# Softmax of the final attention blocks: negated peak as bias of the exponential and per-head sums on ScalarE, with a new order table for those blocks

## The reference, cut to what matters

```
x = x + xattn(layernorm(x), ctx)           # 6 layers, 4 batches
x = x + attn(layernorm(x), ...)
x = x + ffn(layernorm(x), ...)

# attn, for each batch
scores  = einsum('bhse,bhte->bhst', q, k) / sqrt(8) + causal
weights = softmax(scores, axis=-1)
attn    = einsum('bhst,bhte->bshe', weights, v)

# ffn: c carries from batch to batch
ft = sigmoid(xt @ wf.T + c @ uf.T + bf);  it = sigmoid(...);  gt = tanh(...)
c  = ft * c + it * gt
```

## Time and profile before

| | |
|---|---|
| runs | 2611.82, 2612.84, 2605.08 us |
| profiled execution | 2607.36 us, span 2605.6 us |
| PE busy | 2482.2 us (95% of the span), 12652 matmuls |
| DVE busy | 2238.7 us (86%) |
| ACT busy | 2042.3 us (78%) |
| POOL busy | 604.8 us (23%) |
| granted TensorE clock | 0.976 of full over the span |

### The profile page before, as it was taken

One profiled execution on the slowest core, in us unless ns is written; L12 is line 12 of the kernel. 1 busy time (PEld: TensorE's weight loads), 2 busy tenths in 40 slices (PEclk: granted clock), 3 DMA queues, 4 the chain that ended last, 5 costly groups with the idle time before them and its releaser, 6 DMA issues.

```text
span 2605.6 us, 37962 instructions
## 1 busy us (share of the span) xinstructions
PE 2482.2 (95%) x12652; PEld 1522.6 (58%) x12652; DVE 2238.7 (86%) x4427; ACT 2042.3 (78%) x3861; POOL 604.8 (23%) x392
## 2 busy tenths in 40 slices
PE   4799999999999999999999999999999999999876
PEld 2456656656656656656666666566566566565554
DVE  6689898898898898898898898898988988988875
ACT  2588888888888888888888888888888888888531
POOL 3312312212213213213123123123122122131000
PEclk8799999999999999999999999999999999999986
DMA  3000010001001001001001001001001001000000
GB/s 129 25 9 17 25 36 17 25 9 38 25 7 46 17 9 47 9 17 52 9 17 46 9 17 52 9 17 46 9 17 52 9 17 46 9 1 26 1 1 5
DMA packets 16573, 63.56 MB, mean 24 GB/s; under 512 B 2241, under 2 KB 7410, under 8 KB 11642
## 3 DMA queue, kind: packets, MB, share of 16 engines
q1 hardware_dynamic: 16378, 61.13, 7.3%
HBM read 48.25 MB, written 0.29 MB: 19 GB/s over the span
## 4 chain that ended last, share of the span: by engine, by line
PE 58%; DVE 17%; ACT 13%; issue 8%; POOL 3%; DMA 0%; SPq 0%; ACTq 0%; DVEq 0%; POOLq 0%
PE psS L1052 16%; PE psO L1100 9%; PE psO L1101 9%; PE psO L1103 9%; ACT P L890 6%; ACT PH L887 5%; DVE PL L636 4%; PE psL L1146 3%; PE psL L1157 2%; PE psL L1052 2%; DVE back_x L709 1%; ACT qraw L909 1%; POOL back_rstd L422 1%; DVE V L686 1%; PE psA L1203 1%
## 5 line engine op out<-in xcount | busy, mean ns | idle before, releaser
L887 ACT ACTIVATE PH<-psS 128x512 fp32r<-128x512 f32 x1536 | 1009.4, 657 | 177.3 <-PE psS L1052 158.7
L636 DVE TENSOR_TENSOR PL<-P,PH 128x512 fp32r<-128x512 f32 x1536 | 1038.5, 711 | 94.5 <-ACT P L890 84.6
L890 ACT ACTIVATE P<-psS 128x512 f32<-128x512 f32 x1536 | 1009.3, 657 | 108.5 <-DVE PL L636 108.3
L1052 PE MATMUL psS<-QT,KT 128*128 128x512 f16 x3072 | 927.5, 384 | 0.5 <-ACT P L890 0.5
L1100 PE MATMUL psO<-PH,V 128*128 128x512 f32 x1536 | 876.4, 571 | 0.0
L1101 PE MATMUL psO<-PH,VL 128*64 128x512 f32 x1536 | 606.7, 395 | 0.0
L1103 PE MATMUL psO<-PL,V 128*128 128x512 f32 x1536 | 605.9, 394 | 0.1
L1052 PEld LDWEIGHTS psS<-QT,KT 128*128 128x128 f16 x3072 | 216.2, 100 | 368.4 <-issue 281.1
L1100 PEld LDWEIGHTS psO<-PH,V 128*128 128x128 f32 x1536 | 292.2, 190 | 178.0 <-ACT PH L887 9.8
L1103 PEld LDWEIGHTS psO<-PL,V 128*128 128x128 f32 x1536 | 288.1, 188 | 152.1 <-DVE PL L636 0.8
L422 POOL TENSOR_TENSOR rn<-ssc,neghalf 128x16 f32<-128x16 f32 (+2 forms) x73 | 240.7, 3298 | 347.6 <-DVE ssc L571 265.7
(11 more groups left out here) (365 smaller groups left out, 2835.0 us busy)
## 6 DMA issues: line engine op xcount, KB each, us to landing
ctx_sb<-ctxT SPq DMA_DIRECT2D x24, 1024.0 KB, 4.7
KT<-KT SPq DMA_DIRECT2D x48, 256.0 KB, 3.5
W<-wpack SPq DMA_DIRECT2D x6, 1280.0 KB, 5.3
W<-wpack SPq DMA_DIRECT2D x6, 1088.0 KB, 7.3
W<-wpack SPq DMA_DIRECT2D x6, 576.0 KB, 5.7
KT<-biasM SPq DMA_DIRECT2D x1, 1024.0 KB
W<-tail_w SPq DMA_DIRECT2D x1, 832.0 KB
P<-biasW SPq DMA_DIRECT2D x1, 512.0 KB
```

The lines of the kernel that those rows point to most:

```text
L636: nc_v.tensor_tensor(PL[:, here, :], P[:, t % PSLOTS, :], PH[:, here, :], ALU.subtract).then_inc(sem("p_lo"), 1)
L887: nc_a.activation(PH[:, t % HSLOTS, :], bank, ACT.Exp, scale=SIM_SCALE).then_inc(sem("p_hi"), 1)
L890: nc_a.activation(P[:, t % PSLOTS, :], bank, ACT.Exp, scale=SIM_SCALE).then_inc(sem("ca_exp"), 1)
L1052: ins = mm(bank, keys[part], q, start=(part == 0), stop=(part == 1))
```

## The change

The arithmetic stays the same. In the mask stage the subtraction over 128 x 512 goes, and a small instruction negates the four peaks (128 x 4) in its place. The exponential of a chunk, one instruction over 128 x 512 before, becomes four of 128 x 128, one a head; each takes its negated peak as bias and gives the row sum as accumulated output. The four sum stages are replaced by one, `sums`, which waits for the last exponential of the block and takes the reciprocal.

```diff
                         link(nc_v.tensor_reduce(t.peak[:, 4 * c:4 * c + 4], t.s[c], AX_X, ALU.max))
-                        nc_v.tensor_tensor(t.s[c], t.s[c], t.peak[:, 4 * c:4 * c + 4].unsqueeze(2).broadcast_to([128, 4, N]), ALU.subtract).then_inc(sem("t_sub"), 1)
+                        nc_v.tensor_scalar(t.peak[:, 4 * c:4 * c + 4], t.peak[:, 4 * c:4 * c + 4], -1.0, None, ALU.mult).then_inc(sem("t_peak"), 1)
...
-                def sums(c):
-                    def stage():
-                        dve.wait_ge(sem("t_exp"), t.b * 4 + c + 1)
-                        link(nc_v.tensor_reduce(t.sum[:, 4 * c:4 * c + 4], t.s[c], AX_X, ALU.add))
-                        if c == 3:
-                            link(nc_v.reciprocal(t.inv[:], t.sum[:]))
-                    return stage
+                def sums():
+                    dve.wait_ge(sem("t_exp"), t.b * 4 + 4)
+                    link(nc_v.reciprocal(t.inv[:], t.sum[:]))
...
             def tail_exp(t, c):
                 def stage():
-                    act.wait_ge(sem("t_sub"), t.b * 4 + c + 1)
-                    nc_a.activation(t.s[c], t.s[c], ACT.Exp).then_inc(sem("t_exp"), 1)
+                    act.wait_ge(sem("t_peak"), t.b * 4 + c + 1)
+                    for h in range(4):
+                        i = 4 * c + h
+                        ins = nc_a.activation(t.s[c][:, h, :], t.s[c][:, h, :], ACT.Exp, bias=t.peak[:, i:i + 1], accum_out=t.sum[:, i:i + 1])
+                    ins.then_inc(sem("t_exp"), 1)
                 return stage
```

The waits of TensorE's scores and transposes on `t_sub` become waits on `t_peak`. The rest is the four tables, in which many stages of t0, t1, u and v have new steps. One line of `PLAN_PE` as an example:

```diff
-            8: ["u_turn_fin"], 10: ["s_table"], 11: ["t0_turn_fin", "u_proj"], 12: ["f_kv2"], 13: ["f_kv3", "t0_proj"],
...
+            7: ["t0_turn_fin"], 8: ["u_turn_fin"], 10: ["s_table", "t0_proj"], 11: ["u_proj"], 12: ["f_kv2"], 13: ["f_kv3"],
```

More of the change, by code:

```diff
@@ L251, in build @@
             0: ["s_bias"], 2: ["f_turn_sa"], 3: ["f_proj_sa", "f_proj_sa2"], 5: ["f_kv0"], 6: ["f_kv1", "s_null"],
-            8: ["u_turn_fin"], 10: ["s_table"], 11: ["t0_turn_fin", "u_proj"], 12: ["f_kv2"], 13: ["f_kv3", "t0_proj"],
-            14: ["b_wo"], 15: ["u_turn_y2", "t0_turn_y2"], 16: ["t0_qkv"], 18: ["f_turn_q_sa", "b_turn", "u_qkv"],
-            20: ["t1_turn_fin", "f_turn_k_sa", "b_gate", "f_sn"], 21: ["t0_s0"],
[8 rows of a table removed]
-            63: ["f_turn_q_ca", "t1_turn_z"], 64: ["b_down"],
-            65: ["v_turn_fin", "v_proj", "v_turn_y2", "v_qkv", "v_gates2", "v_s0", "v_s1", "v_s2", "v_s3", "v_turn0", "v_turn1", "v_turn2", "v_turn3", "v_pv0", "v_pv1", "v_pv2", "v_pv3", "v_turn_o", "v_wo", "v_turn_z", "v_gates3"],
+            7: ["t0_turn_fin"], 8: ["u_turn_fin"], 10: ["s_table", "t0_proj"], 11: ["u_proj"], 12: ["f_kv2"], 13: ["f_kv3"],
+            14: ["b_wo", "t0_turn_y2"], 15: ["u_turn_y2"], 18: ["f_turn_q_sa", "b_turn", "t0_qkv", "u_qkv"],
[9 rows of a table added]
+            63: ["f_turn_q_ca", "t1_turn_z"], 64: ["b_down"], 65: ["u_turn_z", "v_gates2"],
+            66: ["v_turn_fin", "v_proj", "v_turn_y2", "v_qkv", "v_s0", "v_s1", "v_s2", "v_s3", "v_turn0", "v_turn1", "v_turn2", "v_turn3", "v_pv0", "v_pv1", "v_pv2", "v_pv3", "v_turn_o", "v_wo", "v_turn_z", "v_gates3"],
         }
@@ L275, in build @@
+            43: ["t1_back0"], 47: ["t1_back2"], 50: ["u_gates1"], 53: ["f_raw_ca", "f_sq_ca"], 55: ["f_KT"], 59: ["f_hi_ca"],
+            63: ["f_QT_ca"], 65: ["v_gates2", "v_exp0", "v_exp1", "v_exp2", "v_exp3", "v_back0", "v_back2", "v_gates3"],
         }
         PLAN_DVE = {
-            0: ["s_bias", "f_begin", "f_norm_sa", "f_xnT_sa"], 1: ["e_null"], 2: ["s_null"],
-            5: ["b_spread3", "b_invert3", "b_widen3", "f_V0"], 6: ["f_V1"], 7: ["t0_largest", "u_largest"], 8: ["f_ss_sa"],
@@ L279, in build @@
-            9: ["t0_final", "u_final", "b_scale3"], 10: ["s_turned", "s_table"], 11: ["f_V2", "f_unit_sa", "t0_in"],
-            12: ["u_in"], 13: ["f_null", "f_V3", "t0_norm", "b_out", "t0_gain"], 14: ["u_norm"],
[12 rows of a table removed]
+            0: ["t0_largest", "f_begin", "s_bias", "f_norm_sa", "f_xnT_sa"], 1: ["e_null"], 2: ["s_null"],
[14 rows of a table added]
             45: ["f_invert3", "f_widen3", "t0_cols", "f_scale3"], 47: ["e_scale1", "t1_back3", "f_out"],
-            48: ["t0_res", "f_xnT_ca"], 50: ["u_out", "s_rows"], 51: ["t0_z"], 54: ["e_spread2", "f_ss_ca"],
@@ L295, in build @@
[L295 to L297 removed]
+            48: ["t0_res", "f_xnT_ca"], 50: ["s_rows"], 51: ["t0_z"], 52: ["u_out"], 54: ["e_spread2", "f_ss_ca"],
[3 rows of a table added]
@@ L298, in build @@
         }
         PLAN_POOL = {
[L300 to L303 removed]
+            0: ["f_sa"], 1: ["s_null"], 5: ["t0_fin", "f_rot", "f_sa_q"], 7: ["u_fin"], 8: ["s_mask"], 9: ["f_low_sa"],
@@ L304, in build @@
+            11: ["t0_y"], 12: ["u_y", "t0_y2", "b_out"], 13: ["b_ff"], 14: ["u_y2", "f_kv"], 16: ["t1_fin"],
+            20: ["t1_y", "t1_y2"], 23: ["f_klow"], 26: ["f_out"], 35: ["f_ca"], 36: ["s_rows"], 40: ["f_ca_q"],
+            48: ["f_low_ca"], 54: ["t0_z"], 56: ["t1_z"], 60: ["u_z"], 65: ["v_fin", "v_y", "v_y2", "v_z"],
         }
@@ L845, in on @@
                                base + "gain": attention_gain, base + "own": own, base + "out": attention_out, base + "cols": out_columns,
-                               base + "res": residual, base + "z": z_columns, CELL[t.b] + "_cell" + str(t.b): cell})
+                               base + "res": residual, base + "z": z_columns, base + "sums": sums, CELL[t.b] + "_cell" + str(t.b): cell})
                 for c in range(4):
-                    stages.update({f"{base}key{c}": own_keys(c), f"{base}mask{c}": masked(c), f"{base}sum{c}": sums(c), f"{base}back{c}": turned_back(c)})
+                    stages.update({f"{base}key{c}": own_keys(c), f"{base}mask{c}": masked(c), f"{base}back{c}": turned_back(c)})
             for t in tails:
```

15 lines of the change are left out of this document (3 added, 12 removed), and 53 rows, old and new, of tables (PLAN_ACT, PLAN_DVE, PLAN_PE).

## The result

The changed kernel takes 2588.52 us, median of 5 runs (2587.51 to 2594.97), against 2611.82 us (2605.08 to 2612.93) for the kernel before: a ratio of 0.9921, 95% interval 0.9911 to 0.9932. That is some 21 us less by the ratio and 23 by the medians. Forecast was 2592, with 2583 to 2603 as range. The profiled execution took 2594.97 us, with a span of 2593.3; the one of before took 2607.36. That gap has to be explained too.

The account below looks back on a forecast made before the run. It took VectorE, then TensorE, then a chain from engine to engine as the bound. Gains of 7.5 - 0.5 + 5.2 + 1.8 + 3.0 = 17.0 us gave 2590.4 from the profiled 2607.36; it predicted 2592, range 2583 to 2603.

Parts of the forecast that it names:

- t0 and t1 up to b_up: Window up to 2448.6 us: TensorE's waits for y2 and t0_qkv's columns go; 7.5 us gained, bounds 4 and 10.
- b_up to 2504: Stretch where TensorE is the bound: longer exponentials on ScalarE mostly covered; -0.5 us, bounds +1.3 and -3.
- Block u (a): Start of u: u_largest begins right behind the last PL, so u_in starts 3.0 us sooner, bounds 2 and 3.5.
- Block u (b) and (c): In u: u_gain ahead of b_xnT gives 0.3 us; shorter mask stages less longer exponentials give 1.9.
- (d): In u: gates1 behind both copies delays cell1, but TensorE's 32 small matmuls cover it: nothing; 1 us if uncovered.
- Into v: From u to v: b_down runs ahead of u_turn_z, so v_largest starts sooner; 1.8 us, bounds 1 and 2.
- Block v: In v: lighter masks, no sums ahead of chunk 1's copy, small matmuls without a wait; 3.0 us, bounds 2 and 3.6.
- Chunk of exponentials: On ScalarE: four exponentials of 128 x 128 take 1.2 us a chunk, 0.6 more than the single instruction.
- A: Rival, 17%: the waits only move; the t0 and t1 window gives 3 us instead of 7.5; 2597 us.
- B: Rival, 13%: the accumulated output is dear, 2.5 us a chunk; 6.6 us less gain, 2598 to 2599 us.
- C: Rival, 10%: moved waits and dear accumulated output together, or stages that cancel; 2602 to 2611 us, no change.
- D: Rival, 3%: slower, as a chunk's four exponentials on ScalarE hold up TensorE's last core steps; 2615 us.

Follow-up runs that it names:

- b_down late: The changed kernel with u_turn_z ahead of b_down and gates2 behind v_qkv again: 2589.58 us, ratio 0.9917 to the kernel before.
- the arithmetic alone: The kernel before with negated peaks as bias and sums from the exponentials, its stages in the old order: 2603.73 us, ratio 0.9974.
- the order alone: The kernel before with its subtraction, whole exponentials and four sums kept, but the new order of stages: 2600.66 us, ratio 0.996.
- sums on VectorE: The changed kernel without accumulated sums; VectorE takes the four sums at the end of a block: 2594.42 us, ratio 0.9933 to the kernel before.
- the two with 26.3 us: Profiles of two changed kernels, one with t0_turn_y2 and t0_qkv at steps 15 and 16 (2590.2 us), one with b_down behind u_turn_z (2589.58 us).
- t0_largest late: The changed kernel with t0_largest at step 7 again instead of step 0: 2593.5 us, ratio 0.9928 to the kernel before.
- warm turns: The changed kernel with an unused 128 x 256 matmul ahead of scores 1 to 3 and turns 2 and 3 of u and v: 2586.12 us.
- fillers: Unused matmuls in TensorE's waits in u and v: the changed kernel with the long set 2582.05 us, the kernel before with it 2607.55 us.

## Why the prediction was right

The total holds: 17.0 us were worked out from one profile, and the two profiles of the changed kernel are 12.3 and 17.3 us below the span of before (2605.6 - 2593.3 and 2605.6 - 2588.3). The medians differ by 21 to 23. The profile of before was one of its shorter executions, 4.5 us below the median. The forecast allowed 1.6 of that (2592 for 2590.4); where its other executions spend the 4.5, no run shows. The terms in turn:

- **t0 and t1 up to b_up, 7.5:** 8.0 to 8.1 measured; the walk gave 8.2. Waits of 2.1 and 3.3 were worked out for t1_turn_fin and t1_turn_y2; they are 2.15 and 2.46 (3.17 in the profile of b_down late). Both moves are needed: either undone costs 2.1 to 2.5 us. b_turn starts at 2411.17 instead of 2417.84, 7.9 sooner against S0, but t0_qkv now stands behind it. The core step behind both comes 7.0 sooner (7.5 worked out), and the half clock ahead of it went with the wait. What the walk didn't have is the 0.79 us that TensorE waits for ScalarE's P.
- **b_up to 2504, -0.5:** wrong, in sign and bound. It is +2.36, where I had allowed +1.3. The step that failed is "TensorE is the bound, with 1.3 us to gain at most". TensorE lost its 1.28 us of idle time whole, and its busy time fell by 1.08, of which 0.44 is t0_turn0 moved ahead of b_up. I have no row for the other 0.6. The 5 chunks on ScalarE held it up nowhere in this stretch, though ScalarE rose to 45.8 us of 55.2. This gain needs both halves of the change: 57.77 us with the arithmetic alone, 57.47 with the order alone, 57.21 with sums on VectorE, 55.20 together. TensorE's waits in the stretch say why (timeline of TensorE: two of the kernel before, one with the arithmetic alone, one with the order alone, one with sums on VectorE):

```profile
2456.38 0.63 PE L1272 MATMUL psL<-C,ctx_sb 128*128 128x128 f32 x4 [0.78 <-ACT ET L991]
2463.39 0.60 PE L1052 MATMUL psS<-QT,KT 128*128 128x512 f16 x2 [0.45 <-ACT P L890]
...
2460.66 0.61 PE L1051 MATMUL psS<-QT,KT 128*128 128x512 f16 x2 [1.19 <-ACT P L886]
...
2466.05 0.63 PE L1270 MATMUL psL<-C,KT 128*128 128x128 f32 x4 [1.00 <-DVE KT L793]
...
2450.75 1.10 PE L1259 MATMUL psL<-kraw,W 128*128 128x512 f32 x2 [1.78 <-DVE tail_peak L793]
```

  Before, both waits are for ScalarE. With the arithmetic alone the 0.78 stays and the wait for P grows to 1.19: in the old order the longer exponentials do hold TensorE up. The new order takes both away, but with the old arithmetic, or with the sums alone left on VectorE, TensorE waits there for VectorE.
- **Block u (a), 3.0:** 3.02, and 2.9 when undone alone. (The prediction's "6.5, not 8.8" mixes two starts: from the start of the last PL it is 6.50 against 9.52, from its end 5.8 against 8.8.)
- **Block u (b) and (c), 2.2:** 3.0 to 3.5 up to P in the two profiles, and 4.6 in the two with 26.3 us. Own comes 1.0 sooner against u_in, not 0.3; the masks give 3.5 instead of 2.5, as their scores came at full clock; the exponentials and turns behind them cost 1.0, not 0.6.
- **(d), nothing:** right. cell1 waited 2.36 us, and the last copy ended 3.1 us after the last exponential (3.2 worked out). Where the small matmuls took 3.73 us (t0_largest late), the last eight began an estimated 0.3 us behind the end of that copy (P plus 24/32 of 3.73), so the cover is thin at the full clock.
- **Into v, 1.8:** 1.95 to 1.97. v_largest starts 0.85 us after the last instruction of u's norm.
- **Block v, 3.0:** 0.0 and 2.0 in the two profiles, 2.6 with warm turns (25.55 + 4.10 against 32.25). The mechanism was there: the copy of chunk 1 starts 0.31 us after the last exponential. But P comes only 0.8 us sooner in both profiles, not 1.7: the last peak gains 1.85 instead of 2.3, and the exponentials and the turn behind it cost 1.0 instead of 0.6. The rest of the term was sized as if the small matmuls kept their clock.
- **Chunk of exponentials, 1.2:** 1.65. The 0.45 is the read of the accumulator (0.37) and 0.08 for the heads, 1.28 without accumulator. The estimate of 1.27 worked out by the Trainium skill (ScalarE: Activation LUTs, What ACT_TABLE_LOAD costs) is that of the heads without the sums to 0.01.

What I did not have among the terms: TensorE's clock behind the turns. Against the profile of before it cost 2.7 to 3.1 us in u in both profiles, and up to 0.9 in v and 2.5 at the end. The 2.9 us more than forecast between b_up and the last PL paid for the part in u. So the number is right partly by luck, because two misses cancel.

The rivals: A (the waits only move) fell with 8 us by b_up, though a slow stretch did come back behind the wait for t1. B was right that the accumulated output costs something, at 0.37 a chunk and not 1.3. The rule of the Trainium skill that B named (Perfetto Trace Analysis, Optimizing Scalar/DVE Operations) says that larger operations can pay on a saturated engine. The smaller ones here cost ScalarE 5.3 us between b_up and the last PL (45.8 against 40.5), and TensorE waited for none of it there; it waited 0.79 us for ScalarE just ahead of b_up, and 1.19 for 0.45 in the old order. C and D did not come.

What stays open: why an execution loses the clock at P of u, or at the final matmuls, and another of nearly the same program does not. At P of u all three profiles in the old order kept it (P to output 3.77), and of those in the new order without fillers only one did (3.76, t0_largest late). The fillers show that it can be moved, and what it is worth (8 us), not what sets it. Nor is it known where the 3.2 us ahead of S0 come from.

## What to carry to other kernels

Take an instruction off the engine that is waited for and then look at the order: here each half alone gave 7 and 10.5 us, and one gain of 2.4 came only with both. Compare from mark to mark, not end to end, when the clock moves: in two profiles of one kernel eight of ten stretches agreed within 0.5 us while the ends differed by 5. Where a chain hands over from engine to engine and TensorE stands idle in between, its clock belongs among the terms. Fillers in its idle time gave 8 us here and under 5 in the old order; work brought forward from the end gave 1.35 us more in the profile, which the times alone can't confirm.
